# Which exps of a unit GpSimd adds and which a DMA adds, and where TensorE sums the softmax denominators

## The reference, cut to what matters

```python
scores = einsum('bhcq,bhck->bhqk', q, k) * SCALE      # 8 heads, 1024 x 1024 each, head dim 32
attn = softmax(scores, axis=-1)                       # exp(s - max) / sum of the exps
out = einsum('bhqk,bhck->bhcq', attn, v)
out = einsum('oc,bchw->bohw', w_proj, out) + b_proj
return x + out
```

## Time and profile before

| | |
|---|---|
| median of three executions | 516.5 us |
| profiled execution, whole | 514.55 us |
| its span | 512.8 us |
| TensorE busy | 479.3 us, 93% of the span |
| VectorE busy | 360.1 us, 70% |
| ScalarE busy | 273.3 us, 53% |
| GpSimd busy | 217.8 us, 42% |

### The profile page before, as it was taken

How to read it: one execution, slowest core, us unless ns; L and a number is a source line. 1 busy time by engine, 2 the same in 40 slices (tenths; PEclk the granted TensorE clock), 3 DMA queues, 4 the chain that set the end, 5 groups by cost and what they waited for, 6 DMA issues and landing times.

```text
span 512.8 us, 7031 instructions
## 1 busy us (share of the span) xinstructions
PE 479.3 (93%) x2268; PEld 238.7 (47%) x2268; DVE 360.1 (70%) x687; ACT 273.3 (53%) x522; POOL 217.8 (42%) x203
## 2 busy tenths in 40 slices
PE   8799999999989899999999999999999989998996
PEld 6454444443237565444444322664544444432463
DVE  7599888976164568987887823738988787832573
ACT  3138776767514324876766762131777765764032
POOL 8300021001000002898879991000699888896000
PEclk9969999999998998999999999998999999999999
DMA  5330432000000054487944440034457854442002
GB/s 145 56 57 20 137 65 34 1 2 2 1 0 1 15 123 104 82 203 159 207 89 84 83 79 5 1 88 109 92 120 154 182 105 83 84 83 42 1 0 82
DMA packets 16419, 38.18 MB, mean 74 GB/s; under 512 B 4870, under 2 KB 6030, under 8 KB 16256
## 3 DMA queue, kind: packets, MB, share of 16 engines
q1 hardware_dynamic: 11088, 21.72, 17.7%
q0 software_dynamic: 5152, 16.00, 16.9%
q10 hardware_dynamic: 144, 0.02, 0.0%
HBM read 4.76 MB, written 1.05 MB: 11 GB/s over the span
## 4 chain that ended last, share of the span: by engine, by line
PE 68%; DVE 15%; DMA 4%; ACT 4%; issue 3%; SPq 3%; POOL 2%; ACTq 0%; POOLq 0%; DVEq 0%
PE PV L927 15%; PE S L889 15%; PE S L916 11%; DVE max L662 10%; PE S L1037 4%; DMA k_stack<-kL 4%; PE M L943 3%; PE PV L844 2%; PE S L870 2%; DVE rec_sb L692 2%; PE M L870 2%; PE PV L870 2%; PE S L907 2%; PE S L1082 2%; PE PV L863 1%
## 5 line engine op out<-in xcount | busy, mean ns | idle before, releaser
L662 DVE TENSOR_REDUCE max<-S 128x1 f32<-128x512 f32 x384 | 239.8, 669 | 20.8 <-PE S L889 20.6
L514 ACT ACTIVATE E<-S 128x512 f32<-128x512 f32 x384 | 212.6, 601 | 76.2 <-PE S L916 72.2
L450 POOL TENSOR_TENSOR SUMS<-E 128x512 f32<-128x512 f32 x126 | 167.0, 1476 | 123.9 <-ACT E L514 123.8
L889 PE MATMUL S<-k_stack,q_stack 126*128 126x512 f32 x384 | 183.2, 490 | 13.5 <-DVE max L662 8.7
L916 PE MATMUL S<-q_stack,k_stack 128*128 128x512 f32 x384 | 154.6, 411 | 2.7 <-ACT E L514 1.5
L889 PEld LDWEIGHTS S<-k_stack,q_stack 126*128 126x128 f32 x384 | 74.4, 194 | 92.9 <-DVE max L662 64.7
L927 PE MATMUL PV<-E,V 128*32 128x512 f32 x768 | 95.4, 599 | 1.7 <-ACT pv_sb L521 1.7
L916 PEld LDWEIGHTS S<-q_stack,k_stack 128*128 128x128 f32 x384 | 72.6, 191 | 33.3 <-ACT E L514 20.6
L692 DVE RECIPROCAL rec_sb<-den_sb 128x64 f32<-128x64 f32 (+1 forms) x54 | 35.7, 665 | 35.0 <-ACT den_sb L531 35.0
L503 ACT ACTIVATE mHL<-S 4x128 fp32r<-4x128 f32 x48 | 12.6, 263 | 55.2 <-PE S L907 55.2
L927 PEld LDWEIGHTS PV<-E,V 128*32 128x32 f32 x768 | 20.0, 109 | 45.2 <-issue 28.3
(11 more groups left out here) (180 smaller groups left out, 335.5 us busy)
## 6 DMA issues: line engine op xcount, KB each, us to landing
SUMS<-SUMS POOLq DMA_DIRECT2D x30, 512.0 KB, 5.1
k_stack<-kH SPq DMA_DIRECT2D x32, 128.0 KB, 3.0
q_stack<-qH SPq DMA_DIRECT2D x40, 64.0 KB, 2.0
k_stack<-kL SPq DMA_DIRECT2D x16, 128.0 KB, 3.2
q_stack<-qH SPq DMA_DIRECT2D x16, 128.0 KB, 2.3
q_stack<-mHL SPq DMA_DIRECT2D x96, 2.0 KB
q_stack<-qL SPq DMA_DIRECT2D x20, 64.0 KB, 2.0
X<-x_in_dram SPq DMA_DIRECT2D x2, 512.0 KB, 5.5
```

The lines of the kernel that those rows point to most:

```text
L450: pool.tensor_tensor(SUMS[:, slot, :], E[:, E_PLAN[s][0], :], E[:, E_PLAN[s + 1][0], :], ALU.add).then_inc(sum_ready, 1)
L514: act.activation(E[:, slot, :], B[:, ring_of_scores(s) % B_RING, :], ACT.Exp, scale=1.0 if l == 0 else float(HEAD_DIM[l]) ** -0.5).then_in ...
L662: dve.tensor_reduce(max8[:, m % 2, r:r + 1], A[:, n % A_RING, :], AX.X, ALU.max, negate=True).then_inc(a_used, 1)
L889: pe.matmul(A[:, n % A_RING, :], q_stack[0:SHIFT_ROW, slot, q0:q0 + P], k_stack[0:SHIFT_ROW, slot, k0:k0 + HALF], start=True, stop=True).t ...
```

## The change

GpSimd adds only the first three pairs of a unit's exps (`SUMS_U = 3`). For the units 0 to 14 of a layer a DMA of its queue adds the last two exp tiles, read from E, onto pair sums 0 and 1 of the unit, once the last exp is there. Pair sum 2 stays, so TensorE now has three groups a block (k = 0, 1, 2). In blocks 0 to 2 they come one each behind the value bursts of steps 37, 45 and 53, in the order k = 2, 0, 1; in the last block behind the values of step 126 (as before), behind tile 6 and behind tile 7, with the two last exps of unit 15 at the end. The 16 slots of SUMS are handed out by a plan (`sum_plan`), since a unit now holds three of them, and the slots of E with the last two exps of a unit are given back when the DMA has landed.

```diff
+SUMS_U = PAIRS - 1
-DEN_STEP = 49
+DEN_ORDER = (2, 0, 1)
+def two_slots(tile, a, b):
+    lo, hi = min(a, b), max(a, b)
+    return tile[:, lo:hi + 1:hi - lo, :]
...
-                    for k in range(PAIRS):
-                        if j == UNITS_L - 1 and k == PAIRS - 1:
-                            continue
+                    for k in range(SUMS_U):
                         s = TILES * j + 2 * k
-                        slot = sum_slot(j, k)
+                        slot, freed = SUM_PLAN[j, k]
                         pool.wait_ge(e_ready, STEPS * l + s + 2)
...
+                        if freed or l > 1:
+                            pool.wait_ge(den_done, DENS_L * (l - 1) + freed)
...
                     if j < UNITS_L - 1:
-                        pool.wait_ge(sum_ready, sum_count(l, j, PAIRS - 1))
-                        kept, added = sum_slot(j, 0), sum_slot(j, 2)
-                        pool.dma_start(SUMS[:, kept:kept + 2, :], SUMS[:, added:added + 2, :],
+                        s = TILES * (j + 1)
+                        pool.wait_ge(e_ready, STEPS * l + s)
+                        pool.wait_ge(sum_ready, sum_count(l, j, 1))
+                        pool.dma_start(two_slots(SUMS, SUM_PLAN[j, 0][0], SUM_PLAN[j, 1][0]),
+                                       two_slots(E, E_PLAN[s - 2][0], E_PLAN[s - 1][0]),
                                        accum_op=ALU.add).then_inc(sum_dma[j % 2], 16)
...
-                    act.wait_ge(sum_ready, sum_count(l, HEADS_B * (b + 1) - 1, k))
+                    if k < SUMS_U:
+                        act.wait_ge(sum_ready, sum_count(l, HEADS_B * (b + 1) - 1, k))
+                    else:
+                        for j in (HEADS_B * b + 2, HEADS_B * b + 3):
+                            act.wait_ge(sum_dma[j % 2], dma_count(l, j))
...
+            def denominators(l, b, i):
+                last = b == BLOCKS - 1
+                k = i if last else DEN_ORDER[i]
+                if i == 0 and b:
                     pe.wait_ge(den_out, DEN_OUTS * l + b)
...
+                pe.wait_ge(sum_ready, sum_count(l, HEADS_B * b + 3, k))
+                if k < 2:
+                    for j in (HEADS_B * b + 2, HEADS_B * b + (1 if last else 3)):
+                        pe.wait_ge(sum_dma[j % 2], dma_count(l, j))
                 for u in range(HEADS_B):
...
+                if last and i == SUMS_U - 1:
+                    for s in (STEPS - 2, STEPS - 1):
+                        pe.wait_ge(e_ready, STEPS * l + s + 1)
+                        mm = pe.matmul(M[DP * (HEADS_B - 1):, :], ones[:, 0:DP], E[:, E_PLAN[s][0], :], start=False,
+                                       stop=(s == STEPS - 1))
                 mm.then_inc(den_done, 1)
...
                             values(l, b, 2 * k)
                             values(l, b, 2 * k + 1)
-                    if l and s >= DEN_STEP and (s - DEN_STEP) % 32 == 0:
-                        denominators(l, (s - DEN_STEP) // 32, 0)
-                        denominators(l, (s - DEN_STEP) // 32, 1)
+                            if l and k:
+                                denominators(l, b, k - 1)
...
                 for t in range(5, TILES):
-                    if t == TILES - 1 and l:
-                        denominators(l, BLOCKS - 1, 1)
                     values(l, BLOCKS - 1, t)
+                    if t > 5 and l:
+                        denominators(l, BLOCKS - 1, t - 5)
```

More of the change, by code:

```diff
@@ L30 @@
 E_SLOTS = 34
-SUM_UNITS = 6
-SUM_SLOTS = 2 * SUM_UNITS + 4
+SUMS_U = PAIRS - 1
+SUM_SLOTS = 16
 SLOTS = 5
@@ L83, in slot_plan, with sum_plan @@
     return plan
-def sum_slot(j, k):
-    return 2 * (j % SUM_UNITS) + k if k < 2 else 2 * SUM_UNITS + 2 * (j % 2) + k - 2
+def sum_plan():
+    free, done, plan = list(range(SUM_SLOTS)), 0, {}
+    for j in range(UNITS_L):
+        for k in range(SUMS_U):
+            if not free:
+                b, kk = done // SUMS_U, DEN_ORDER[done % SUMS_U]
+                free += [plan[HEADS_B * b + u, kk][0] for u in range(HEADS_B)]
+                done += 1
+            plan[j, k] = (free.pop(0), done)
+    return plan
+def two_slots(tile, a, b):
+    lo, hi = min(a, b), max(a, b)
+    return tile[:, lo:hi + 1:hi - lo, :]
 def attention_chain(nc, x, w0, w1, w2, w3, pos_bias, cols, row3, out):
@@ L241, in slot_of @@
             return h % SLOTS
-        E_PLAN = slot_plan()
-        DENS_L = 2 * BLOCKS
+        E_PLAN, SUM_PLAN = slot_plan(), sum_plan()
+        DENS_L = SUMS_U * BLOCKS
         PAIRS_L = BLOCKS * PAIRS
-        SUMS_L = UNITS_L * PAIRS - 1
+        SUMS_L = UNITS_L * SUMS_U
         def dma_count(l, j):
@@ L251, in sum_count @@
         def sum_count(l, j, k):
-            return (l - 1) * SUMS_L + min(PAIRS * j + k + 1, SUMS_L)
+            return (l - 1) * SUMS_L + SUMS_U * j + k + 1
         REC_L = sum(REC_PARTS)
@@ L527, in denominators_out @@
                 else:
-                    act.wait_ge(den_done, DENS_L * (l - 1) + 2 * (b + 1))
+                    act.wait_ge(den_done, DENS_L * (l - 1) + SUMS_U * (b + 1))
                 if l + b:
@@ L930, in values @@
                     mm.then_inc(pv_done, 1)
-            def denominators(l, b, k):
-                if k == 0 and b:
+            def denominators(l, b, i):
+                last = b == BLOCKS - 1
+                k = i if last else DEN_ORDER[i]
+                if i == 0 and b:
                     pe.wait_ge(den_out, DEN_OUTS * l + b)
[L936 to L941, removed]
-                for u in range(HEADS_B):
[L943 to L949, removed]
+                pe.wait_ge(sum_ready, sum_count(l, HEADS_B * b + 3, k))
+                if k < 2:
+                    for j in (HEADS_B * b + 2, HEADS_B * b + (1 if last else 3)):
+                        pe.wait_ge(sum_dma[j % 2], dma_count(l, j))
+                for u in range(HEADS_B):
+                    mm = pe.matmul(M[DP * u:DP * (u + 1), :], ones[:, 0:DP], SUMS[:, SUM_PLAN[HEADS_B * b + u, k][0], :],
+                                   start=(i == 0), stop=(i == SUMS_U - 1 and not (last and u == HEADS_B - 1)))
+                if last and i == SUMS_U - 1:
[3 more added lines that the diff above has]
+                                       stop=(s == STEPS - 1))
                 mm.then_inc(den_done, 1)
```

## The result

The changed kernel takes 524.72 us, the median of four executions (523.74 to 527.6), against 516.32 for the kernel before (515.22 to 517.43, four). The ratio is 1.0172, with a 95% interval of 1.0126 to 1.0218: slower, by between 1.3% and 2.2%. Its profiled execution took 524.40 us, its span is 522.7 us against 512.8.

The account below looks back on a forecast made before the run. Bound: TensorE and VectorE waiting in order on each other, not GpSimd. 2 x (7.74 - 4.15 + 0.69 - 0.30 + 0.86) - 1.62 = +8.1 us, forecast 524.5 us; own range 521.5 to 527, full range 516 to 529.

Parts of the forecast that it names:

- A group behind a burst costs 0.86 us and passes on in full: Nine value bursts a layer each grow by one group of 0.86 us, paid whole: +7.74 us a layer.
- TensorE waited 0.44 us elsewhere in the interval: Rival's ground: this wait for VectorE absorbs half of each added group, 516.7 us by the median; chance 0.15.
- Three bursts go: Two-group bursts at steps 49, 81, 113 disappear, giving back 1.55, 1.14 and 1.46 us: -4.15 a layer.
- The gain at 49 is taken back by the stack DMA: At step 68 TensorE waits 0.69 us longer for head 7's stack: +0.69 a layer, bounds 0 to about 1.4.
- rival B: Half of each added group absorbed, and step 68's stack waits vanish, 3.3 us more: 513.4 us; chance 0.06.
- ScalarE's 0.40 us: Ahead of step 109, relieving GpSimd frees between nothing and 0.4 us of ScalarE's wait: -0.30 a layer.
- Block 2 behind step 109: Groups added at steps 109 and 117 cost 0.86 us each; the burst dropped at 113 gives back 1.46.
- The last block's first group: Its waits for unit 14's DMA, 0.38 us (layer 1) and 1.24 (layer 2), go: -1.62 for both layers together.
- the end: At a layer's end the reciprocals start 0.86 us later, behind the extra third group: +0.86 a layer.
- rival C: Half-length rows make accumulating DMAs land in up to twice 5.1 us: about 534 us, half gives 529; chance 0.09.
- GpSimd's busy time: Over the whole kernel it falls by some 40 us, with no effect on the end.

## Why the prediction was right

It said 524.5 us and slower; measured were 524.72. The mechanism that carries the sum was right. That the times agree to 0.2 us is partly luck: the terms below miss by more, and the measurement scatters by more.

- *A group behind a burst costs 0.86 us and passes on in full.* Right, shown three ways: VectorE's idle time (1.17 to 2.03), the intervals (+0.85 to +0.88 at 37, 69, 85, 101), and the run without six groups (their intervals fell by 0.83 to 0.86). That VectorE was already idle at that very place was the right row to go by; that TensorE waited 0.44 us elsewhere in the interval was not.
- *Three bursts go.* Right where it could be checked, with the added group in the same interval: 77 to 85 -0.27 and -0.25 against -0.28.
- *The gain at 49 is taken back by the stack DMA.* Right in direction: 45 to 69 gained nothing from it. Its size was short in layer 1 (+1.38 against +0.86) and right in layer 2 (+0.90), and the wait came in two parts, since head 6's stack was late at step 60 as well (0.36 and 0.72 us). At step 68 the 1.9 us that I had named came out in layer 1 (1.92), the 1.4 in layer 2 did not (0.72). In layer 2 the sum is thus right by another way than the one I gave. Whether GpSimd's DMAs make those loads later stays open: the run with neighbouring slots had no wait in layer 1 and 1.66 us in layer 2, and with GpSimd's old work such waits turned up at step 52 (0.50 and 0.69 us in two runs), so single profiles scatter by as much as the question. One thing the runs do settle is the price. From 61 to 69 the interval was 7.20, 7.67, 8.05 and 8.38 us with waits of 0.73, 1.19, 1.58 and 1.92 us, 6.47 and the wait each time; but with no wait it was 6.84 to 6.86 (the two runs with groups at 49 and 57), or 7.31 (neighbouring slots), not 6.47. So a longer wait is paid in full, as I had it, while the first 0.4 us or more of one are free, and rival B's 3.3 us for all waits were too many.
- *ScalarE's 0.40 us.* Wrong, by 0.30 a layer: 101 to 109 grew by the full 0.86. I had misread the row. It named GpSimd as the one that came last, but with GpSimd relieved the same idle time of 0.40 us stood there, ended by TensorE's score tile, and without a group the interval was 6.33 us as before. So GpSimd had been no later there than TensorE.
- *Block 2 behind step 109.* +0.43 and +0.14 against +0.26.
- *The last block's first group.* -0.54 and -1.43 against -0.38 and -1.24, and the end +0.84 against +0.86 (4.58 us from the second group to the reciprocals, 4.6 expected).
- *Longer landings (rival C).* The landing is 5.3 us against 5.1, where C needed up to twice 5.1. GpSimd's issue is 1.08 against 0.88 on average. The last block's first group did not wait for either.
- *GpSimd's busy time.* It fell by 32 us and not by some 40: the sum of the lost additions left out the dearer issues (6 us) and took all additions at their mean. Nothing hangs on it.

The errors in layer 1 (+0.85, most of it the stack waits and ScalarE's 0.30) and the 1.1 us ahead of it make the difference between the profiled spans 9.9 us where I had 8.1; the medians differ by 8.4.

## What to carry to other kernels

Before moving work on a nearly full engine, ask at the new place which other engine is already idle there. Here it was VectorE, and every group put there was paid in full (0.86 us), however much slack TensorE showed elsewhere in the interval (0.44 us). Work that must be added is cheaper where the partner engine has its own extra work (here the reciprocals: 0.01 us for a single group in layer 2), and single pieces need enough steps between them for the ring to fill again (two were too few). Relieving an engine gives nothing where nobody waits for it (here 32 us of GpSimd's time gave only what TensorE had waited ahead of the last block's first group), but making it wait for a buffer when it has no slack costs (5.16 us of waiting became 2.96 us of TensorE's). And a row that names a releaser names the one that came last: ask who would have come next.

## What the runs showed of the hardware

- A group of four 32-column float32 matmuls of 512 columns adds 0.86 us to a burst of its kind (2.78 against 1.92), but a burst of one alone lasts 1.06.
- An accumulating DMA of 512 KB issued by GpSimd had a median landing of 4.6 to 5.1 us in the runs with 1024 elements a row, and of 5.1 to 5.5 us in those where 18 of the 30 had 512 (7456 packets on its queue and not 5152). GpSimd's issue took 0.88 us with 1024 elements a row and 1.20 with 512.
